# Convolution weights made and used in two halves of kernel rows

## The reference, cut to what matters

```python
h = relu(einsum('bchw,oc->bohw', x, pw1_w) + pw1_b)      # pointwise
mask = top_k(sigmoid(fc2(relu(fc1(mean(h before relu))))), 32)   # per image: which channels live
offsets = tanh(mean(h) @ off_w.T + off_b).reshape(B, 3, 2)
sel = (h * mask)[:, :32]
for i, (ksz, base) in enumerate([(3, dw3), (5, dw5), (7, dw7)]):
    w = base[:32] * (1 + sigmoid(offsets[:, i, 0])) + tanh(offsets[:, i, 1])   # per image
    outs.append(depthwise_conv(sel, w, ksz))
out = einsum('bchw,oc->bohw', concatenate(outs), pw_w[:, :96]) + pw_b + x
```

## Time and profile before

| | |
|---|---|
| runs | 315.04, 315.33, 318.14 us; median 315.33 us |
| profiled execution | 313.89 us, of which the span of the trace is 312.1 us |
| PE busy | 267.1 us, 86% of the span |
| DVE busy | 229.1 us, 73% |
| ACT busy | 205.0 us, 66% |
| POOL busy | 158.1 us, 51% |
| convolution matmuls, line 1269 | 528 |

### The profile page before, as it was taken

One profiled execution on the slowest core, in us unless ns is written; L12 is line 12 of the kernel. 1 busy time (PEld: TensorE's weight loads), 2 busy tenths in 40 slices (PEclk: granted clock), 3 DMA queues, 4 the chain that ended last, 5 costly groups with the idle time before them and its releaser, 6 DMA issues.

```text
span 312.1 us, 6648 instructions
## 1 busy us (share of the span) xinstructions
PE 267.1 (86%) x2486; PEld 212.0 (68%) x2486; DVE 229.1 (73%) x448; ACT 205.0 (66%) x331; POOL 158.1 (51%) x195
## 2 busy tenths in 40 slices
PE   1555878899999998999989979999997797899992
PEld 1334655886767777676767745464796687899992
DVE  2767629278788887878888572896999999998222
ACT  6685754576768586695836779987731862897800
POOL 5052545468768676886471716181090990444400
PEclk9985999799999999999999999999999997999997
DMA  6971358334533343343441000560466445699841
GB/s 169 200 164 46 76 128 168 82 78 89 113 77 85 73 103 87 83 109 74 99 93 39 2 0 0 120 141 0 118 108 138 102 94 106 153 185 192 179 78 34
DMA packets 35118, 31.06 MB, mean 100 GB/s; under 512 B 20816, under 2 KB 30032, under 8 KB 35088
## 3 DMA queue, kind: packets, MB, share of 16 engines
q1 hardware_dynamic: 30608, 23.55, 32.9%
q0 software_dynamic: 3392, 6.17, 11.4%
q10 hardware_dynamic: 1088, 0.94, 1.3%
HBM read 4.54 MB, written 2.10 MB: 21 GB/s over the span
## 4 chain that ended last, share of the span: by engine, by line
PE 33%; POOL 19%; DVE 19%; issue 12%; ACT 8%; SPq 5%; DMA 4%; DVEq 0%; POOLq 0%; ACTq 0%
PE psum L1269 11%; POOL parts L339 8%; POOL k_blocks L556 5%; PE psum L1008 4%; PE psum L1072 4%; PE psum L1171 4%; POOL q_blocks L564 4%; SPq L451 3%; DMA k_heads<-k_parts 2%; PE psum L929 2%; ACT conv_w L858 2%; DVE maxima L1422 2%; SPq L463 2%; POOL q_heads L391 1%; PE psum L1188 1%
## 5 line engine op out<-in xcount | busy, mean ns | idle before, releaser
L1269 PE MATMUL psum<-shifted,conv_w 128*128 128x286 f32 x528 | 73.8, 300 | 5.4 <-issue 3.0
L1269 PEld LDWEIGHTS psum<-shifted,conv_w 128*128 128x128 f32 x528 | 71.8, 193 | 6.4 <-issue 4.4
L1008 PE MATMUL psum<-q_heads,k_blocks 128*128 128x256 f32 x384 | 62.8, 303 | 3.7 <-ACT probs L716 2.0
L1008 PEld LDWEIGHTS psum<-q_heads,k_blocks 128*128 128x128 f32 x384 | 52.1, 192 | 14.4 <-issue 6.3
L1422 DVE TENSOR_REDUCE maxima<-psum 128x8 f32<-128x512 f32 x64 | 40.3, 680 | 5.5 <-PE psum L982 5.5
L716 ACT ACTIVATE probs<-psum 128x512 f32<-128x512 f32 x64 | 37.6, 605 | 10.2 <-PE psum L1008 9.2
L556 POOL DMA_DIRECT2D k_blocks<-k_parts x56 | 32.3, 584 | 6.9 <-PE psum L1008 6.9
L339 POOL TENSOR_TENSOR conv_w<-whole_w,conv_w 128x1408 fp32r<-128x1408 f32 x6 | 19.5, 3252 | 31.2 <-ACT conv_w L852 31.2
L339 POOL TENSOR_TENSOR parts<-x,parts 128x256 fp32r<-128x256 f32 (+1 forms) x21 | 19.3, 932 | 27.9 <-ACT parts L665 20.8
L339 POOL TENSOR_TENSOR parts<-square_logvar,parts 128x512 fp32r<-128x512 f32 x13 | 19.0, 1460 | 28.4 <-ACT square_logvar L729 15.7
L929 PE MATMUL psum<-parts,center_average 128*128 128x512 f32 x64 | 23.5, 450 | 10.1 <-DVE parts L339 8.1
(11 more groups left out here) (154 smaller groups left out, 504.3 us busy)
## 6 DMA issues: line engine op xcount, KB each, us to landing
shifted<-images SPq DMA_DIRECT2D x32, 243.8 KB, 4.7
q_heads<-q_parts SPq DMA_DIRECT2D x128, 32.0 KB
k_blocks<-k_parts POOLq DMA_DIRECT2D x56, 64.0 KB, 2.5
k_heads<-k_parts SPq DMA_DIRECT2D x64, 32.0 KB, 2.3
out<-x SPq DMA_DIRECT2D x8, 256.0 KB, 3.0
q_blocks<-q_parts POOLq DMA_DIRECT2D x28, 64.0 KB, 2.5
conv_w<-conv_w SPq DMA_DIRECT2D x10, 176.0 KB, 3.8
x<-in_x SPq DMA_DIRECT2D x6, 256.0 KB, 5.0
```

The costliest lines, as they stand in the source:

```text
L1008: ins = pe.matmul(bank[:, hh * G // 2:(hh + 1) * G // 2], k_blocks[:, hh, w // (NW // 2), k_part, w % (NW // 2), :], q_heads[:, w // (NW / ...
L1269: ins = pe.matmul(psum[:, CONV[bh][g], 0:SPAN], conv_w[bh][:, w_part, h * NSLOT + slot, :], shifted[:, bh, part, stream, first:first + SPA ...
```

## The change

The weights of a unit are made, rounded, copied and subtracted in two halves (kernel rows h = 0 and 1), each with its own semaphore step, so all counts double (`dv_whole`, `ac_high`, `ac_odd_high`, `low_weights`). From unit 2 on PE runs the high passes of half 0, then waits for half 1. All products of size 5 go into one PSUM bank (`product5_bank`), for all units.

Orders change too. On PE, `gate_scores(2)` comes behind the low passes of unit 1 and `gate_spread(2)` behind those of unit 2. On DVE, `result(0, 1)` comes ahead of `gate_mask(2)`, and `result(1, 0)` between the two halves of unit 4. On POOL, the low images 4 to 6 come earlier and 7 waits for the end of gate 1. On SP, the order of images, low moves and stores is written out anew.

```diff
-            for i in range(NB4 - 1):
-                for bh in range(2):
-                    sp.wait_ge(S["pe_conv"], 2 * i + bh + 1)
-                    copy_images(i + 1, bh)
-                    store(i, bh)
-                    move_low(2 * i + bh + 2, bh, (1, 2))
-            for bh in range(2):
-                store(NB4 - 1, bh)
+            def next_images(u):
+                sp.wait_ge(S["pe_conv"], u - 1)
+                copy_images(u // 2, u % 2)
+
+            next_images(2)
+            next_images(3)
+            move_low(2, 0, (1, 2))
+            store(0, 0)
+            next_images(4)
+            move_low(3, 1, (1, 2))
+            store(0, 1)
+            next_images(5)
+            move_low(4, 0, (1, 2))
+            store(1, 0)
+            for u in range(6, B):
+                move_low(u - 1, (u - 1) % 2, (1, 2))
+                next_images(u)
+                store((u - 3) // 2, (u - 3) % 2)
+            move_low(B - 1, 1, (1, 2))
+            for u in range(B - 3, B):
+                store(u // 2, u % 2)
...
-            for n in range(4):
+            for n in range(6):
                 low_image(n, n // 2, n % 2)
             pool.wait_ge(S["pe_mlp1"], 4 * NG)
             no_row(1)
-            pool.wait_ge(S["dv_whole"], 2)
-            for n in range(4, 6):
-                low_image(n, n // 2, n % 2)
+            low_image(6, 3, 0)
+            pool.wait_ge(S["gate_dve"], 2 * GATE_STEPS)
+            low_image(7, 3, 1)
             for u in range(2, B):
...
+                for h in range(2):
+                    pool.wait_ge(S["ac_high"], 2 * u + h + 1)
+                    low_half(pool, u % 2, h).then_inc(S["low_weights"], 1)
...
             def high_weights(u, bh):
-                even_high(u, bh)
-                odd_high(u, bh)
-                odd_low(u, bh)
+                even_high(u, bh, 0)
+                odd_high(u, bh, 0, (0, 1))
+                even_high(u, bh, 1)
+                odd_high(u, bh, 1, (0, 1, 2))
...
             def high_passes(b4, bh):
                 high_weights_in(b4, bh)
                 for g in range(3):
-                    passes(bh, 0, g)
+                    passes(bh, 0, g, range(1))
+                pe.wait_ge(S["ac_odd_high"], 4 * b4 + 2 * bh + 2)
+                for g in range(3):
+                    passes(bh, 0, g, range(1, 2))
...
             passes(1, 0, 2)
+            low_passes(0, 1)
             gate_scores(2)
-            low_passes(0, 1)
-            high_weights_in(1, 0)
-            passes(0, 0, 0)
+            high_passes(1, 0)
+            low_passes(1, 0)
             gate_spread(2)
-            passes(0, 0, 1)
-            passes(0, 0, 2)
-            low_passes(1, 0)
             high_passes(1, 1)
...
+            def whole_half(b4, bh, h):
                 u = 2 * b4 + bh
+                w, base = whole_w[:, bh, h:h + 1], 4 * (2 * u + h)
+                if u == 0:
+                    dve.wait_ge(S["dv_fuse"], 1)
+                if u > 1:
+                    dve.wait_ge(S["low_weights"], 2 * (u - 1))
+                dve.tensor_tensor(product5_bank, *factors(b4, bh, 1, h), ALU.mult)
+                dve.tensor_tensor(product3[:, h:h + 1], *factors(b4, bh, 0, h), ALU.mult)
+                dve.tensor_tensor(taps_window(w, 2), *factors(b4, bh, 2, h), ALU.mult).then_inc(S["dv_product"], 1)
+                dve.wait_ge(S["dv_product"], base + 1)
+                middle = product5_bank[:, :, 2:5, :]
+                dve.tensor_tensor(middle, middle, product3[:, h:h + 1], ALU.add).then_inc(S["dv_product"], 1)
+                dve.wait_ge(S["dv_product"], base + 2)
                 window = taps_window(w, 1)
+                dve.tensor_tensor(window, window, product5_bank, ALU.add).then_inc(S["dv_product"], 1)
+                dve.wait_ge(S["dv_product"], base + 3)
...
             gate_means(2)
-            whole_weights(1, 0)
+            whole_half(1, 0, 0)
             gate_hidden(2)
+            whole_half(1, 0, 1)
             result(0, 0)
             gate_scores(2)
-            products(1, 1)
+            whole_half(1, 1, 0)
             gate_spread(2)
-            add_products(1, 1)
+            whole_half(1, 1, 1)
+            result(0, 1)
             gate_mask(2)
-            result(0, 1)
             gate_taps(2)
-            for b4 in range(2, NB4):
-                for bh in range(2):
-                    whole_weights_by_banks(b4, bh)
-                    result(b4 - 1, bh)
+            whole_half(2, 0, 0)
+            result(1, 0)
+            whole_half(2, 0, 1)
+            for u in range(5, B):
+                for h in range(2):
+                    whole_half(u // 2, u % 2, h)
+                result((u - 2) // 2, u % 2)
```

More of the change, by code:

```diff
@@ L846, in gate, with even_high, odd_high @@
                 act.activation(mem["shift"], mem["offset"], ACT.Tanh).then_inc(S["gate_act"], 1)
-            def even_high(u, bh):
-                act.wait_ge(S["dv_whole"], u + 1)
+            def even_high(u, bh, h):
+                act.wait_ge(S["dv_whole"], 2 * u + h + 1)
                 if not (isinstance(u, int) and u < 2):
                     act.wait_ge(S["pe_conv"], u - 1)
-                act.copy(conv_w[bh][:, 0, :, 0:C], whole_w[:, bh].rearrange("p h t c -> p (h t) c")).then_inc(S["ac_high"], 1)
-            def odd_high(u, bh, moves=range(3)):
-                act.wait_ge(S["ac_high"], u + 1)
+                act.copy(conv_w[bh][:, 0, h * NSLOT:(h + 1) * NSLOT, 0:C], whole_w[:, bh, h]).then_inc(S["ac_high"], 1)
+            def odd_high(u, bh, h, moves):
+                act.wait_ge(S["ac_high"], 2 * u + h + 1)
                 for m in moves:
-                    to, of = odd_rows(bh, 0, m)
+                    to, of = odd_rows_half(bh, m, h)
                     ins = act.copy(to, of.bitcast(F32))
@@ L899, in _ @@
             relu(4, 2, 0)
+            even_high(0, 0, 0)
             gelu(7, 1)
-            even_high(0, 0)
+            even_high(0, 0, 1)
             relu(5, 2, 1)
-            odd_high(0, 0, range(1))
+            odd_high(0, 0, 0, (0,))
+            odd_high(0, 0, 1, (0,))
             relu(6, 3, 0)
@@ L906, in _ @@
             relu(7, 3, 1)
-            even_high(1, 1)
-            odd_high(1, 1, range(1))
+            even_high(1, 1, 0)
+            even_high(1, 1, 1)
+            odd_high(1, 1, 0, (0,))
+            odd_high(1, 1, 1, (0,))
             keep_shared(0, 0)
-            even_high(2, 0)
-            odd_high(2, 0)
+            high_weights(2, 0)
+            keep_shared(1, 1)
             gate(2)
             odd_low(2, 0)
-            keep_shared(1, 1)
             high_weights(3, 1)
+            odd_low(3, 1)
             with act.Fori(2, NB4) as b4:
@@ L1259, in _, with passes @@
             gate_scores(1)
-            def passes(bh, w_part, g):
+            def passes(bh, w_part, g, rows=range(NKT // TAP)):
                 stream, tiles = SUBFILTERS[g]
                 last = NKT // TAP * len(tiles) - 1
-                for i, (h, (slot, column)) in enumerate((h, tile) for h in range(NKT // TAP) for tile in tiles):
+                for i, (h, (slot, column)) in enumerate(((h, tile) for h in rows for tile in tiles), rows[0] * len(tiles)):
                     first = h * (SHIFTS // 2) * PITCH + column
@@ L1681, in whole_weights @@
[L1681 to L1683 removed]
             def low_weights(b4, bh):
[L1686 to L1687 removed]
+                for h in range(2):
+                    dve.wait_ge(S["ac_high"], 4 * b4 + 2 * bh + h + 1)
+                    low_half(dve, bh, h).then_inc(S["low_weights"], 1)
@@ L1718, in _ @@
             add_mlp(4)
-            products(0, 0)
+            whole_half(0, 0, 0)
             add_mlp(5)
-            add_products(0, 0)
+            whole_half(0, 0, 1)
             gate_means(1)
@@ L1726, in _ @@
             gate_hidden(1)
-            products(0, 1)
+            whole_half(0, 1, 0)
             gate_scores(1)
-            add_products(0, 1)
+            whole_half(0, 1, 1)
             gate_spread(1)
```

78 lines of the change are left out of this document (23 added, 55 removed).

## The result

The changed kernel is **slower**: median 320.52 us (four runs, 317.79 to 322.06) against 315.19 us for the kernel before (four runs), a ratio of 1.0175 (95% interval 1.0119 to 1.023). The profiled execution of the changed kernel took 319.60 us with a span of 317.4 us, 5.3 us more than the span before. All of that lies in the stage of the convolutions, from the first of its 528 matmuls to the end of the last: before 221.31 to 306.43 us, 85.1 us; after 221.17 to 311.83 us, 90.7 us.

The account below looks back on a forecast made before the run. Bound: PE's waits before 271.26 us (7.7 us) and lost clock (1.7 us). Without clock -2.1 us, two falls +3.4 us: profiled 313.89 becomes 315.2 us, median 316.6 us; range 310.5 to 319.8 us.

Parts of the forecast that it names:

- three falls, or a later landing: Rival: low clock after each wait behind `next_images`, or moves landing at 9.7 us; up to +5.1 us, 320.4 us; chance 0.27.
- Unit 1 ends sooner: PE, unit 1: low passes no longer behind `gate_scores(2)`, end at 241.8 us, plus 0.4 us for a later `gate_spread(1)`.
- T1: End of unit 1 on PE, forecast at 242.2 us.
- The landing: SP's low moves, queued behind the next images, let low passes of units 2 to 4 start 9.0 us after the preceding unit's end.
- The falls behind these waits: PE's clock drops to its lower level after two of three waits for low moves, 1.7 us each, +3.4 us.
- Unit 2's high passes: PE, unit 2: result of unit 0 ready at 242.2 us, high passes 242.3 to 248.2 us; priced at nothing.
- The price of a doubled instruction: DVE: 0.13 us fixed per instruction, seven doubled cost 0.9 us per unit; the skill's formula gave 0.16 and 1.1 us.
- Unit 3's wait of 2.96 us gone: PE before unit 3: DVE has `result(0, 1)` ready by about 251.5 us, which removes the 2.96 us wait.
- Unit 4's second half: PE, unit 4: high half 0 ends at 269.0 us, ACT's half 1 comes at 269.9 us, a wait of 0.9 us.
- T3: End of unit 3 on PE, forecast at 266.0 us.
- Units 5 to 7: PE's last units keep 8.79 us each; DVE's 7.9 and ACT's 7.1 us per unit stay below, so halving costs nothing.
- Halving gains only in unit 4: PE starting on half weights helps only unit 4; elsewhere images, results or PE itself are later than the weights.

Follow-up runs that it names:

- f1: Changed kernel with 14 extra matmuls on PE before `gate_spread(1)`, into an unused bank; median 317.38 us, ratio 1.0117 to the kernel before.
- e1: Changed kernel with low image 6 on POOL waiting, like 7, for the end of gate 1; median 318.15 us, ratio 1.0081 to the kernel before.
- e2: Changed kernel with SP's low moves of units 2 to 4 ahead of the images of units 3 to 5; median 316.50 us, ratio 1.0037 to before.
- e4: Kernel before, whole weights kept, with only SP's order of the changed kernel; median 318.60 us, ratio 1.0054 to the kernel before.
- f3: Changed kernel with low moves first on SP and images 6 and 7 just ahead of units 3 and 4's low weights; median 313.65 us, ratio 0.9945.
- e3: Changed kernel with both low image 6 late and low moves ahead of the next images; stage 82.6 us, median 316.64 us, ratio 0.9902 to before.
- f2: Kernel e3, but PE waits for both halves of the high weights before a unit's high passes; median 321.44 us, ratio 1.0236 to before.

## Why the prediction was wrong, step by step

I forecast 316.6 us; 320.52 was measured, 3.9 more, above the range. The time is that of the rival "three falls, or a later landing" (320.4 us), but not by its mechanism: landings were as forecast, and the third fall wasn't behind `next_images`.

- **"Unit 1 ends sooner" failed.** T1 was to be 242.2 us and was 246.6. The term that failed is the 0.4 us (ends 0 and 1.3) by which `gate_spread(1)` holds PE: it held it 2.34 us and brought a fall, for which I had no term. I priced the doubled instructions of DVE (0.9 us) and took from the moved images only a gain, since they leave gate 1. Where images 4 and 5 and image 6 would go instead I never laid beside DVE's rows: image 6 met DVE's halves of unit 1, on the path to `gate_spread(1)`. That DVE is held by POOL stood in my own text, as the 2.62 us of line 1617; I used it in one direction, and wrongly: that instruction is in gate 2 and waited for the low weights of unit 3 (254.22 us), not for images 4 and 5. f1 splits the loss: 2.3 us of wait, 2.9 of clock; e1 takes it away.
- **The landing, right.** 9.0 us from the end of a unit; 8.7, 9.3 and 8.8 measured. The waits were to be 3.0, 2.5 and 2.2 us and were 2.45, 2.48 and 2.82. e2 shows that the order is the cause, and e4 that it costs 2.0 us even without halves. In the changed kernel it costs 3.8 us of the stage (e2, behind unit 1).
- **The falls behind these waits, right**: two, 3.0 us in all, for 3.4. The third, 6.8 us long and 2.9 us dear, belongs to the failed step.
- **Unit 2's high passes, right by luck**: their start doesn't wait, but the result of unit 0 was there at 246.7 us and not at 242.2. T1, as late, hid it. In e1, with T1 mended, PE waits 2.74 us for it, and f3 shows that images 6 and 7 beside DVE were the cause: the same omission again.
- **The price of a doubled instruction, right in sum, wrong in the reading.** Two half blocks take 2 x 2.90 us (241.71 to 244.61 us is one) for 4.85, 0.95 us more, as forecast. But 128 elements take 0.29 us (line 1686) and 512 take 0.69 (line 1661 of before), so 1.04 ns per element and 0.16 us fixed, the estimate that I set aside for 0.13; instructions in a row overlap by a little, which is why the sum came out.
- **Unit 3's wait of 2.96 us gone, right.** Unit 4's second half (0.9 us) wasn't waited for, since T3 was late; in e2 and e3, where T3 is not, the wait is 2.5 us, and I had it too small.
- **Units 5 to 7, right**: 220 matmuls in 30.86 us, a fall included, no wait.
- **"Halving gains only in unit 4", half right.** As the changed kernel stands the images and moves hide it; with these mended f2 puts it at about 5 to 9 us of a run, 3.8 of them waits.

The sum put right: -2.1 (forecast without clock) + 4.4 (T1) - 0.2 (landings) + 3.0 (two falls) = +5.1 us; the stage shows +5.5. How many falls a sum has to carry I guessed throughout. Two for three waits was fair: in the stage of the twelve profiles 18 of the 23 waits from 2.1 us up were followed by a fall, and none of the ten from 1.0 to 1.9 us.

## What to carry to other kernels

Work that is moved off one place on a shared path lands on another: lay every moved POOL instruction beside DVE's rows at its new place, those with two SBUF inputs first, but one-input ones too, and ask who waits. In an in-order queue put what PE needs next ahead of anything that waits for PE. And price a wait of 2 us and more on TensorE with a second term, the clock that may fall behind it.

## What the runs showed of the hardware

- A DVE instruction of 0.29 us was held for 2.72 us, through three POOL instructions in a row (0.73, 0.72, 1.20 us); I had reckoned with one at most. Two inputs aren't needed: line 1587, one input of 2 elements, took 0.60 us beside image 7 (234.84 us); in the kernel before, with POOL idle, the same line (1562) took 0.16 at 235.07 us.
- Behind waits from 2.1 us up the clock fell 18 times of 23, behind ten waits from 1.0 to 1.9 us never in this stage (ahead of it, at 54 us, it did after 1.5). Among the longer ones, up to 2.8 us, length doesn't tell. Behind 2.34, 2.48 and 2.82 us it fell in the changed kernel, behind 2.45 it did not; in e1 it fell behind 2.74 us, in e3 at the same place and the same 2.74 us it did not. In e4 it fell behind 2.25 us at `gate_scores(2)`, in the kernel before behind the same wait it did not.
- A fall lasted 3.4 us fifteen times and 6.8 us three times: once behind `gate_spread(1)` in the changed kernel, twice in f2. In e2, behind the same wait at `gate_spread(1)`, it was 3.4 us.
